# Attention on one Trainium2 core: GpSimd's sums, gathers and the loads in another order, and the row maxima turned by VectorE in 32x32 blocks and written by eight transfers

## The chip, the cores and the metric

The kernel runs on one core of a Trainium2 chip. The metric is the device time of one execution in microseconds. Measured three times, the kernel before took 1709.15 us in the median (1704.74 to 1709.72). A difference of 0.3% is about 5 us.

## The reference

Sixteen batches of 512 tokens with 256 features go through a layer norm, and three things are added: the input, block-sparse attention of the normed input, and a mixture of experts (16 experts, the two best for each token) with a shared expert.

```python
xn = _layernorm(x)                                   # x: [16, 512, 256]
qkv = (xn @ qkv_w.T)...                              # 16 heads of 16 features
block_mask = (c >= thresh) | eye(M)                  # M = 8 blocks of 64 tokens
scores = where(tmask, einsum('bhqd,bhkd->bhqk', q, k) * SCALE, -inf)
out = einsum('bhqk,bhkd->bhqd', softmax(scores), v)
x + (out @ proj_w.T + proj_b) + (routed + shared)
```

## The kernel before

There are three phases. `phase_front` norms the input, computes the shared expert, and sorts the tokens by expert. `phase_experts` computes the routed experts into `scratch_y`. `phase_attention` does the rest, and the change lies in it alone. It takes the time from about 590 us to the end.

**The unit of work.** A batch has 16 heads, in four groups (`q`) of four. A group is walked in eight steps (two heads and 128 tokens each), so a batch has 32 steps, `j` = 0 to 31. At a step TensorE makes two things. `st_pair` (L1599) multiplies keys with queries, transposed, for step j; ScalarE takes the exponential of it (`exp_pair`, L1409), and TensorE's `pv` (L1613) multiplies that with the values. `s_pair` (L1587) makes plain scores for the group two ahead; VectorE takes their row maxima (`max_pair`, L1449), 1024 columns at a time. Both use the three PSUM tiles of `ring` in turn.

**The row maxima.** The maxima have to be subtracted inside `st_pair`. So the query operand `stack[0]` has two rows more (`TOP0`, `TOP0 + 1`), the high and the low part of the maximum of each query, against rows of minus one on the key side. The maxima come out of VectorE with a query on each partition, and must lie along the free dimension of those two rows. Before, TensorE transposes them (`top_by_query`, L1555, 16x128 into the shared PSUM tile `ps_work`), VectorE splits them into two parts (`take_top`, L1458 and L1460), and two transfers of 8 KB write them into the stack (`top_rows`, L1201). The list `WORK` says at which step TensorE does which side job in `ps_work`: projections of the next batch (`qk`, `v`), the output by token (`o`), its transposition (`turn`), the output projection of the batch before (`final`) and the maxima (`top`, at j = 2, 10, 18, 26). Each job waits until the one before it has been taken out of `ps_work`.

**The queues.** Each engine's program is written out by hand in its order. SyncE (SP) issues nearly all transfers, in the order of its `body`: a transfer whose wait isn't over holds back all behind it. Once a batch SP does `store_out` of the batch before (L1207), then `load_part` (L1213, L1214), which first waits until that store has landed because it fills the same tile `part`, then `load_x`, and then `top_rows` for the first group of the next batch. GpSimd (POOL) splits q and k into two parts (`split`, L1299, L1301), does the same with the output (`split_on`, L1311, L1313), widens the mask (`widen`, L1284), gathers the experts' rows (`gather_y`, L1331, eight a batch), and adds them up (`add_y`: two weightings, L1339, and four sums into `part`, L1349). VectorE's `add_final` (L1484) waits for all six, and then adds the output projection.

```python
                if not first:
                    store_out(b - 1)
                    load_part(b)
                if not isinstance(b, int) or b + 2 < B:
                    load_x(b + 2)
                if not last:
                    top_rows(b + 1, d, 0)
```

The bodies of batches 0 to 3 and 13 to 15 are written out, those between are in a loop of three. The functions that the change touches:

## Time and profile before

| | |
|---|---|
| median of three runs | 1709.15 us (1704.74 to 1709.72) |
| the profiled execution's own time | 1708.7 us |
| its span in the profile | 1706.7 us |
| TensorE (PE) busy | 1383.7 us, 81% |
| VectorE (DVE) busy | 1035.2 us, 61% |
| ScalarE (ACT) busy | 868.0 us, 51% |
| GpSimd (POOL) busy | 781.8 us, 46% |
| mean granted TensorE clock | 0.912 |

The span is the time from the first to the last instruction. PEld is TensorE's loading of weights, beside the matmuls. A row of a group names the line, the engine, the operation, the tiles written and read, the count, the busy time with the mean of one in ns, and then the idle time of the engine before such instructions with what ended it. SPq is SyncE's issuing.

### The profile page before, as it was taken

Reading aid. Unit: us, or ns where it says so; the run is one execution under the profiler, and the core shown is the slowest. Engines: PE = TensorE matmul, PEld = TensorE weight load, DVE = VectorE, ACT = ScalarE, POOL = GpSimd, SP = SyncE. Lnnn points to the kernel's source line nnn. Section 1 sums busy time; section 2 is a strip of 40 time slices with the busy share of each in tenths; the row PEclk is TensorE's granted clock in tenths of the full one; section 3 lists DMA queues with packets and bytes.
Section 4 is the critical chain, followed back from the end, with each engine's and each line's share of the span. In section 5 each row is a group of like instructions: output and inputs, shape, how many; then the busy total and the mean of one; then the engine's idle time right before and its main releaser. Section 6 shows DMA issues by size and latency. Waiting matters only on the chain.

```text
span 1706.7 us, 28417 instructions
## 1 busy us (share of the span) xinstructions
PE 1383.7 (81%) x8618; PEld 812.8 (48%) x8619; DVE 1035.2 (61%) x1560; ACT 868.0 (51%) x1168; POOL 781.8 (46%) x778
## 2 busy tenths in 40 slices
PE   4988872398888647999898898899898898898984
PEld 3766651388888623443343343344343443443432
DVE  6876552455545408776676676676676776666660
ACT  4444420355555303666565565566565566555662
POOL 2577775022222321365364463463562663652645
PEclk9998985599999857999999999999998999998996
DMA  4666543344444355454554454445435635535411
GB/s 176 236 242 237 207 164 129 124 145 149 158 148 149 125 136 213 148 201 150 176 196 162 174 184 177 175 146 215 173 140 173 221 136 202 186 123 199 175 47 53
DMA packets 119722, 284.59 MB, mean 167 GB/s; under 512 B 16768, under 2 KB 52736, under 8 KB 111424
## 3 DMA queue, kind: packets, MB, share of 16 engines
q1 hardware_dynamic: 101568, 230.75, 38.8%
q0 software_dynamic: 18048, 52.45, 8.8%
q8 instruction: 64, 1.05, 0.2%
q14 instruction: 42, 0.34, 0.1%
HBM read 152.98 MB, written 129.11 MB: 165 GB/s over the span
## 4 chain that ended last, share of the span: by engine, by line
PE 21%; POOL 15%; DMA 14%; SPq 6%; issue 4%; ACT 2%; DVE 2%; POOLq 0%; DVEq 0%; ACTq 0%; another core or an unknown queue 0%
POOL at_part L1349 8%; DMA out<-at_part 8%; PE at_ps_pv L1613 7%; PE at_ring L1599 5%; PE at_ps_work L699 5%; DMA at_stack<-at_top_part 5%; POOL at_yg L1339 4%; PE at_ring L1587 3%; SPq L1168 2%; ACT at_pt L1409 1%; DVE at_top L1449 1%; DMA scratch_stack<-at_qk_part 1%; SPq L1222 1%; POOL at_qk_part L1301 1%; SPq L1201 1%
## 5 line engine op out<-in xcount | busy, mean ns | idle before, releaser
L1449 DVE TENSOR_REDUCE at_top<-at_ring 128x2 f32<-128x1024 f32 x512 | 624.7, 1223 | 321.2 <-PE at_ring L1587 295.1
L1409 ACT ACTIVATE at_pt<-at_ring 128x1024 f32<-128x1024 f32 x512 | 522.8, 1027 | 344.3 <-PE at_ring L1599 313.7
L1599 PE MATMUL at_ring<-at_stack 58*128 58x512 f32 x1024 | 260.8, 507 | 58.4 <-DMA at_stack<-at_top_part 51.3
L1613 PE MATMUL at_ps_pv<-at_pt,at_vx 128*32 128x512 f32 x2048 | 284.0, 628 | 4.4 <-ACT at_pt L1409 4.2
L1587 PE MATMUL at_ring<-at_stack 56*128 56x512 f32 x1024 | 228.7, 443 | 57.0 <-ACT at_pt L1409 25.1
L1599 PEld LDWEIGHTS at_ring<-at_stack 58*128 58x128 f32 x1024 | 98.1, 188 | 292.6 <-issue 196.8
L1331 POOL DMA_INDIRECT at_yg<-scratch_y,at_stage x128 | 123.5, 965 | 208.9 <-ACT at_pt L1409 174.9
L803 POOL DMA_DIRECT2D scratch_y<-ex_y x72 | 52.4, 727 | 223.0 <-ACT ex_y L841 219.0
L1299 POOL CAST at_qk_part<-at_qk_raw 128x512 fp32r<-128x512 f32 x64 | 39.2, 612 | 251.1 <-ACT at_qk_raw L1381 226.3
L284 POOL DMA_INDIRECT scratch_xs<-fr_xn,fr_slot x128 | 126.4, 988 | 56.0 <-issue 35.9
L1587 PEld LDWEIGHTS at_ring<-at_stack 56*128 56x128 f32 x1024 | 102.1, 196 | 96.8 <-ACT at_pt L1409 54.2
L699 PE MATMUL at_ps_work<-at_xh,qkv_part 128*128 128x512 f32 x256 | 106.7, 459 | 17.2 <-DMA at_xl<-scratch_xp 12.4
L880 DVE TENSOR_TENSOR ex_xl<-ex_ps_x,ex_xh 128x512 fp32r<-128x512 f32 x72 | 49.8, 691 | 80.9 <-ACT ex_xh L825 80.9
L699 PE MATMUL fr_ps_out<-fr_wd_part,fr_hh 128*128 128x256 f32 x256 | 57.0, 321 | 43.5 <-POOL fr_hl L276 41.5
L699 PE MATMUL ex_ps_gu<-ex_w_part,ex_xh 128*128 x288 | 88.3, 307 | 1.0 <-DVE ex_xl L880 0.7
L1301 POOL TENSOR_TENSOR at_qk_part<-at_qk_raw,at_qk_part 128x512 fp32r<-128x512 f32 x64 | 82.1, 1282 | 5.1
L699 PE MATMUL ex_ps_gu<-ex_w_part,ex_xl 128*128 x288 | 82.5, 287 | 0.0
L699 PE MATMUL ex_ps_gu<-ex_w,ex_xh 128*128 x288 | 82.4, 286 | 0.0
L1613 PEld LDWEIGHTS at_ps_pv<-at_pt,at_vx 128*32 128x32 f32 x2048 | 40.8, 109 | 86.9 <-issue 79.9
L1381 ACT COPY at_qk_raw<-at_ps_work 128x512 f32<-128x512 f32 x64 | 37.5, 587 | 85.9 <-PE at_ps_work L699 85.9
L699 PEld LDWEIGHTS at_ps_work<-at_xh,qkv_part 128*128 128x128 f32 x256 | 53.8, 210 | 57.4 <-DVE at_top_part L1460 16.0
L1349 POOL TENSOR_TENSOR at_part<-at_part,at_yg 128x1024 f32<-128x1024 f32 x32 | 76.2, 2383 | 2.5
(204 smaller groups left out, 2463.3 us busy)
## 6 DMA issues: line engine op xcount, KB each, us to landing
at_stack<-scratch_stack SPq DMA_DIRECT2D x64, 1024.0 KB, 6.3
scratch_stack<-at_qk_part SPq DMA_DIRECT2D x192, 256.0 KB, 2.6
ex_xg<-scratch_xs SPq DMA_DIRECT2D x144, 128.0 KB, 2.1
scratch_y<-ex_y POOLq DMA_DIRECT2D x72, 256.0 KB, 3.1
fr_x_in<-in_x SPq DMA_DIRECT2D x16, 512.0 KB
scratch_xp<-fr_xh SPq DMA_DIRECT2D x16, 512.0 KB
scratch_xp<-fr_xl SPq DMA_DIRECT2D x16, 512.0 KB
scratch_part<-fr_part SPq DMA_DIRECT2D x16, 512.0 KB
```

Of the source, the lines that this page charges most:

```text
L284: nc.gpsimd.indirect_dma_start(out=dram["xs"], out_offset=bass.IndirectOffsetOnAxis(ap=slot[:, j, c:c + 1], axis=0), in_=xn[b % XN][:, t, ...
L699: ins = nc.tensor.matmul(out, a, b, start=(first and n == 0), stop=(last and n == len(todo) - 1))
L803: nc.gpsimd.dma_start(dram["y"][bass.ds(at, 2 * P), :].rearrange("(u p) d -> p u d", p=P), y[i][:]).then_inc(y_stored[i], 16)
L1301: nc.gpsimd.tensor_tensor(qk_part[s][1][:], qk_raw[s][:], f32(qk_part[s][0][:]), ALU.subtract).then_inc(split_ready, 1)
L1331: nc.gpsimd.indirect_dma_start(out=yg[j][:, t, :], out_offset=None, in_=dram["y"], in_offset=bass.IndirectOffsetOnAxis(ap=stage[:, j, t:t ...
L1339: nc.gpsimd.tensor_tensor(yg[j][:], yg[j][:], keep["weight"][:, j, bass.ds(TB * b, TB)].unsqueeze(2).broadcast_to([P, TB, D]), ALU.mult).t ...
L1349: nc.gpsimd.tensor_tensor(part[:], part[:], term, ALU.add).then_inc(added, 1)
L1409: nc.scalar.activation(pt[t][:, 2 * pair:2 * pair + 2, :], st_slot(c, j)[:], ACT.Exp, scale=float(HD) ** -0.5).then_inc(exp_ready, 1)
L1449: v.tensor_reduce(cols[:, :, TB * pair + t], slot[0][:], AX, ALU.max).then_inc(s_max, 1)
L1587: last = nc.tensor.matmul(slot[:, half, :], stack[0][r][rows, pl, t * P:(t + 1) * P], stack[1][r][rows, pl, :], start=True, stop=True)
L1599: last = nc.tensor.matmul(slot[:, half, :], stack[1][r][rows, pl, t * P:(t + 1) * P], stack[0][r][rows, pl, :], start=True, stop=True)
L1613: last = nc.tensor.matmul(ps_pv[2 * HD * g:2 * HD * (g + 1), :], vx[c][:, t, G * q + g, :], pt[t][:, g, :], start=(t == 0), stop=(t == TB ...
```

## The change

- The maxima no longer go through TensorE. `turn_top` on VectorE splits the [128, 16] tile into high and low (128x16 each), and turns the [128, 32] result in 32x32 blocks (one instruction). It comes right after the eighth maximum of a group. The block form leaves pieces of 32 queries, so `top_rows` now issues eight transfers of 128-byte pieces instead of two of 512-byte ones.
- `WORK` loses its four `top` entries a batch.
- `load_x` has three buffers and is moved up, behind the first stack load. `load_part` loses the load of x, which becomes `load_rows`, one batch ahead. `store_mask` and `widen` are moved from the batch's start to the end of the batch before.
- On GpSimd the four sums into `part` are split up: x and the bias are added to the first gathered tile (`add_x`) within the same batch, and only one weighting and two sums are left for the next batch's start. The gathers are spread between the other work.

```diff
+    TOPS = 16 * 2 * (P // 32)
-    WORK = ((1, "qk", 0), (2, "top", 0), (3, "qk", 1), (5, "o", 0), (7, "turn", 0), (9, "turn", 1), (10, "top", 1),
...
+    WORK = ((1, "qk", 0), (3, "qk", 1), (5, "o", 0), (7, "turn", 0), (9, "turn", 1), (11, "qk", 2), (13, "o", 1),
...
-        xh, xl = sb("xh", [P, KD, N], F32R), sb("xl", [P, KD, N], F32R)
+        xh = [sb(f"xh{i}", [P, KD, N], F32R) for i in range(RING)]
+        xl = [sb(f"xl{i}", [P, KD, N], F32R) for i in range(RING)]
...
             def top_rows(b, c, q):
-                sp.wait_ge(top_low, ready)
+                sp.wait_ge(turned, ready)
                 pairs = slice((q % 2) * 2, (q % 2) * 2 + 2)
                 for x in range(2):
-                    sp.dma_start(f32(stack[0][group(c, q)][TOP0 + x::64, pairs, :]).rearrange("e r n -> e (r n)"),
-                                 f32(top_part[q % 2][:, x, :])).then_inc(top_here[q % 2], 16)
+                    for a in range(P // 32):
+                        rows = 32 * a + G * TB * x
+                        sp.dma_start(f32(stack[0][group(c, q)][TOP0 + x::64, pairs, :]).rearrange(
+                            "e r (t a n) -> e (r t) a n", t=TB, a=P // 32)[:, :, a],
+                            top_turned[q % 2][rows:rows + G * TB]).then_inc(top_here[q % 2], 16)
...
             def body(b, c, first=False, last=False):
                 d = (c + 1) % 3
+                counts = mask_counts(b + 2)
                 top_rows(b, c, 1)
                 if not last:
-                    store_mask(b + 1, d)
                     store_qk(b + 1, d, 0)
                     store_qk(b + 1, d, 1)
                     load_stack(b + 1, d, 0)
+                if not isinstance(b, int) or b + 2 < B:
+                    load_x(b + 2, (c + 2) % 3)
                 top_rows(b, c, 2)
...
                 if not first:
                     store_out(b - 1)
-                    load_part(b)
+                load_part(b)
+                if not last:
+                    load_rows(b + 1)
                 if not isinstance(b, int) or b + 2 < B:
-                    load_x(b + 2)
+                    store_mask(b + 2, (c + 2) % 3, counts)
                 if not last:
                     top_rows(b + 1, d, 0)
...
+                if not first:
+                    weigh_y(b - 1, 1)
                 if not last:
-                    widen(b + 1)
                     split(b + 1, 0)
+                if not first:
+                    add_y(b - 1, 1)
+                if not last:
                     split(b + 1, 1)
                 if not first:
+                    add_y(b - 1, 0)
                     split_on(b - 1, 0)
+                stage_rows(b)
+                gather_y(b, 0, 0, 8)
+                if not first:
                     split_on(b - 1, 1)
-                    add_y(b - 1)
+                gather_y(b, 0, 1, 11)
                 if not last:
                     split(b + 1, 2)
+                gather_y(b, 0, 2, 14)
+                gather_y(b, 0, 3, 15)
+                if not last:
                     split(b + 1, 3)
-                gather_y(b)
+                weigh_y(b, 0)
+                add_x(b)
+                gather_y(b, 1, 0, 20)
+                if not isinstance(b, int) or b + 2 < B:
+                    widen(b + 2)
+                for t in range(1, TB):
+                    gather_y(b, 1, t, 20 + 3 * t)
...
-            def take_top(u, q, past_use):
+            def turn_top(u, q, past_use):
                 i = q % 2
-                dve.wait_ge(top_in_psum, u + 1)
+                dve.wait_ge(s_max, HALF * u + HALF)
+                if past(u, 2):
+                    dve.wait_ge(turned, u - 1)
+                v.tensor_copy(top_part[i][:, 0, :], top[i][:]).then_inc(top_high, 1)
+                dve.wait_ge(top_high, u + 1)
+                v.tensor_tensor(top_part[i][:, 1, :], top[i][:], f32(top_part[i][:, 0, :]), ALU.subtract).then_inc(top_low, 1)
                 if past_use is not None:
                     dve.wait_ge(top_here[i], past_use)
...
+                dve.wait_ge(top_low, u + 1)
+                v.transpose(top_turned[i][:], f32(top_part[i][:]).rearrange("p x c -> p (x c)")).then_inc(turned, 1)
```

How the rows stand on the engines. First SP's queue, from the store of a batch's output on; the row of L1201 holds the maxima of two groups, two transfers each. Before:

```order
L1193 DMA at_stack<-scratch_stack 128x2048 x2
L1207 DMA out<-at_part 128x1024
L1213 DMA at_part<-scratch_part 128x1024
L1214 DMA at_x_in<-in_x 128x1024
L1153 DMA at_xh<-scratch_xp 128x1024
L1153 DMA at_xl<-scratch_xp 128x1024
L1201 DMA at_stack<-at_top_part 2x8x128 x4
L1181 DMA scratch_stack<-at_wide 32x512 x4
L1168 DMA scratch_stack<-at_qk_part 64x2x512 x6
```

The same place of the changed kernel:

```order
L1205 DMA at_stack<-scratch_stack 128x2048 x2
L1222 DMA out<-at_part 128x1024
L1228 DMA at_part<-scratch_part 128x1024
L1235 DMA at_x_in<-in_x 128x1024
L1193 DMA scratch_stack<-at_wide 32x512 x4
L1215 DMA at_stack<-at_top_turned 2x8x32 x16
L1175 DMA scratch_stack<-at_qk_part 64x2x512 x6
L1205 DMA at_stack<-scratch_stack 128x2048 x2
L1160 DMA at_xh<-scratch_xp 128x1024
L1160 DMA at_xl<-scratch_xp 128x1024
L1215 DMA at_stack<-at_top_turned 2x8x32 x8
```

Between the store and the first group's maxima, the two loads of the next x have gone and the four of the mask have come; the maxima are eight transfers to a group.

Next GpSimd at the start of a batch, from the first split of the next batch's queries on. Before:

```order
L1299 CAST at_qk_part<-at_qk_raw 128x512
L1301 TENSOR_TENSOR at_qk_part<-at_qk_raw,at_qk_part 128x512
L1299 CAST at_qk_part<-at_qk_raw 128x512
L1301 TENSOR_TENSOR at_qk_part<-at_qk_raw,at_qk_part 128x512
L1311 CAST at_on_part<-at_on_raw 128x512
L1313 TENSOR_TENSOR at_on_part<-at_on_raw,at_on_part 128x512
L1311 CAST at_on_part<-at_on_raw 128x512
L1313 TENSOR_TENSOR at_on_part<-at_on_raw,at_on_part 128x512
L1339 TENSOR_TENSOR at_yg<-at_yg,weight 128x1024 x2
L1349 TENSOR_TENSOR at_part<-at_part,at_x_in 128x1024
L1349 TENSOR_TENSOR at_part<-at_part,at_bias 128x1024
L1349 TENSOR_TENSOR at_part<-at_part,at_yg 128x1024 x2
```

And now:

```order
L1363 TENSOR_TENSOR at_yg<-at_yg,weight 128x1024
L1325 CAST at_qk_part<-at_qk_raw 128x512
L1327 TENSOR_TENSOR at_qk_part<-at_qk_raw,at_qk_part 128x512
L1382 TENSOR_TENSOR at_part<-at_part,at_yg 128x1024
L1325 CAST at_qk_part<-at_qk_raw 128x512
L1327 TENSOR_TENSOR at_qk_part<-at_qk_raw,at_qk_part 128x512
L1382 TENSOR_TENSOR at_part<-at_part,at_yg 128x1024
L1337 CAST at_on_part<-at_on_raw 128x512
L1339 TENSOR_TENSOR at_on_part<-at_on_raw,at_on_part 128x512
L1348 COPY at_stage<-slot 128x8
L1355 DMA at_yg<-scratch_y,at_stage 128x256
```

Six long operations behind the splits of the output have become three ahead of them; the other three stand later in the batch before.

## Rows read from the trace of the kernel before

**Rows 1.** The page: span and busy time of each engine.

```profile
span 1706.7 us, 28417 instructions
PE 1383.7 (81%) x8618; PEld 812.8 (48%) x8619; DVE 1035.2 (61%) x1560; ACT 868.0 (51%) x1168; POOL 781.8 (46%) x778
```

**Rows 2.** Windows, batches 1 to 14: us, busy times, granted clock, DMA share, GB/s.

```profile
714.28:1625.00 910.72, 813.09 (x4986) 369.93 (x4986) 621.80 (x701) 538.10 (x618) 465.57 (x430) 0.95 0.49 174
```

**Rows 3.** Waits of the same stretch: us in total, times, the longest.

```profile
PE at_ring L1599 <- DMA at_stack<-at_top_part: 51.3, 12, 6.9
DVE at_part L1484 <- POOL at_part L1349: 21.1, 14, 1.6
DVE at_top L1449 <- remote: 17.6, 9, 2.2
PE at_ps_work L699 <- DVE at_top_part L1460: 9.8, 17, 0.7
```

**Rows 4.** Timeline of SP's queue at the end of batch 8: start, us.

```profile
1214.52 1.38 SPq L1193 DMA_DIRECT2D at_stack<-scratch_stack  x2
1216.11 0.42 SPq L1207 DMA_DIRECT2D out<-at_part  x1
1225.87 0.34 SPq L1213 DMA_DIRECT2D at_part<-scratch_part  x1
...
1227.83 1.09 SPq L1201 DMA_DIRECT2D at_stack<-at_top_part  x2
```

**Rows 5.** The chain that ended last, at the same place: start, us.

```profile
1216.11 9.61 DMA out<-at_part
1228.41 6.50 DMA at_stack<-at_top_part
```

**Rows 6.** Timeline of PE, the first step of batch 9.

```profile
1234.95 0.50 PE L1599 MATMUL at_ring<-at_stack 58*128 58x512 f32 x2 [3.41 <-DMA at_stack<-at_top_part]
```

**Rows 7.** Window just behind that wait, columns as in rows 2.

```profile
1237.50:1239.50 2.00, 2.00 (x7) 1.16 (x6) 1.12 (x1) 1.34 (x2) 0.00 (x0) 0.51 0.03 8
```

**Rows 8.** Timeline of ACT: exponentials of j = 0 and 2, batches 9 and 11.

```profile
1235.58 1.03 ACT L1409 ACTIVATE at_pt<-at_ring 128x1024 f32<-128x1024 f32 x1 [3.21 <-PE at_ring L1599]
1241.06 1.03 ACT L1409 ACTIVATE at_pt<-at_ring 128x1024 f32<-128x1024 f32 x1
1366.36 1.02 ACT L1409 ACTIVATE at_pt<-at_ring 128x1024 f32<-128x1024 f32 x1 [1.08 <-PE at_ring L1599]
1370.31 1.03 ACT L1409 ACTIVATE at_pt<-at_ring 128x1024 f32<-128x1024 f32 x1
```

**Rows 9.** Groups by line: sums, weightings, the maxima's transposition, small VectorE operations.

```profile
L1349 POOL TENSOR_TENSOR at_part<-at_part,at_yg 128x1024 f32<-128x1024 f32 x32 | 76.2, 2383 | 2.5
L1339 POOL TENSOR_TENSOR at_yg<-at_yg,weight 128x1024 f32<-128x1024 f32 x32 | 59.9, 1894 | 1.8 <-DMA at_yg<-scratch_y,at_stage 1.8
L1555 PE MATMUL at_ps_work<-ident,at_top 128*16 128x128 f32 x64 | 17.8, 278 | 8.9 <-DVE at_part L1484 7.2 <-DVE at_top L1449 1.6
L1458 DVE CAST at_top_part<-at_ps_work 16x128 fp32r<-16x128 f32 x64 | 17.7, 276 | 5.0 <-remote 2.2 <-PE at_ps_work L1555 1.2
L452 DVE TENSOR_TENSOR fr_carry<-fr_carry,fr_upto 128x16 f32<-128x16 f32 x8 | 1.5, 190 | 0.3
```

**Rows 10.** Issues by line on SP: ns least/median/most.

```profile
L1201 SPq DMA_DIRECT2D at_stack<-at_top_part x128: 495/532/618, 650.9 to 1658.9; - x128
L1222 SPq DMA_DIRECT2D scratch_stack<-at_block_of x6: 882/1288/1303, 598.0 to 616.1; - x6
```

**Rows 11.** Timeline of SP's queue: the masks of one batch.

```profile
1244.32 1.74 SPq L1181 DMA_DIRECT2D scratch_stack<-at_wide  x4
```

**Rows 12.** The page's DMA issues: KB each, us to landing.

```profile
scratch_stack<-at_qk_part SPq DMA_DIRECT2D x192, 256.0 KB, 2.6
```

**Rows 13.** Timelines of POOL and PE after the last step.

```profile
1678.70 3.75 POOL L1339 TENSOR_TENSOR at_yg<-at_yg,weight 128x1024 f32<-128x1024 f32 x2 [1.83 <-DMA at_yg<-scratch_y,at_stage]
...
1696.13 2.90 PE L699 MATMUL at_ps_work<-proj_part,at_on_part 128*128 128x256 f32 x12 [11.76 <-POOL at_on_part L1313]
```

161 lines of the change are left out of this document (84 added, 77 removed).

## The prediction

> **What bounds the kernel now.** I read the page first: TensorE (PE) is busy for 81% of the span [rows 1]. Within batches 1 to 14 it is 813 of 911 us, or 89% [rows 2], VectorE 68% and GpSimd 51%. A batch takes 910.72 / 14 = 65.05 us. So TensorE is the bound inside a batch, and about 98 us of these 911 are its own gaps. The waits tell what ends the gaps [rows 3]: TensorE waits 51.3 us, in 12 batches of 14, for the maxima's transfer into the stack at a batch's first step. VectorE waits 21.1 us, 14 times, for GpSimd's sums before it can add the output projection; meanwhile no row maxima are taken. TensorE waits 9.8 us for VectorE to clear the transposed maxima out of the shared tile. The 17.6 us that VectorE waits for "remote" are no work of this program's engines, and I leave them as they are.
>
> Why the maxima come late is read from SP's queue and the chain. In batch 8 the store of the output is issued at 1216.11, and the load behind it stands until 1225.87 [rows 4], since the store takes 9.61 us to land [rows 5]. Four loads follow, 2 MB together, and only then, at 1227.83, the maxima [rows 4]. These 8 KB transfers land 6.50 us after 1228.41 [rows 5]: the ring works in order, and they queue behind the loads. TensorE has then stood 3.41 us [rows 6]. Right afterwards its granted clock is 0.51, the 1.2 GHz level [rows 7], so that the first two steps take 1241.06 - 1235.58 = 5.48 us in batch 9; in batch 11, where ScalarE waited only 1.08 us, the same two take 1370.31 - 1366.36 = 3.95 us [rows 8].
>
> **The change, part by part.** All sums are made against the profiled execution, 1708.7 us, which is 0.45 us under the median of the three; I treat them as the same.
>
> *A, the wait at the batch's start: -51.3 us* [rows 3]. This is the whole of it; what comes back is F.
>
> *B, the slow clock behind it: -18 us.* 5.48 - 3.95 = 1.53 us [rows 8], 12 times.
>
> *C, the sums before the output projection: -17 us.* Before, a weighting pair and four sums take 2 x 1.89 + 4 x 2.38 = 13.3 us [rows 9] behind `split_on`. Now 1.89 + 2 x 2.38 = 6.7 us stand at the batch's start, spread between the splits, and the output projection is at j = 17, about 30 us into the batch. Their finish should lie near 13 us (weighting, split, sum, split, sum). So the 21.1 us go; I take four fifths, because part of such a wait is slack for TensorE. The other 6.7 us move to the middle of the batch before. GpSimd's cover is large (51% busy), and its gathers need their rows only at the end of the batch.
>
> *D, the transposition off TensorE: -14 us.* Per batch four matmuls of 0.278 us [rows 9] go, 14 x 4 x 0.278 = 15.6 us on the engine that bounds, and the 9.8 us of waits [rows 3]. The bounds are 9.8 and 25.4 us. I take 14, as the side job behind each transposition also loses the switch, but the steps around it wait partly for ScalarE.
>
> *E, the work on VectorE: +8 us.* The old pair is 16x128, 0.276 us the first of them [rows 9], about 0.55 together. The new operations are 128x16, 128x16 and a turn of 128x32. The nearest row is a 128x16 sum of 0.190 us [rows 9], so the three are 0.57 us if the turn costs as much, and 0.66 if it costs the 0.276 of the old cast. By itself that is nothing. But the set stands right behind the eighth maximum, and in steps 5 to 9 VectorE has five maxima, an output and this set in hardly more time than they need. I take 0.6 us a batch, 14 x 0.6 = 8. Bounds: 0, and all of it uncovered, 14 x 4 x 0.65 = 36 us. The Trainium skill ("VectorE: DVE Perf Modes", The three transpose paths) says that VectorE turns 32x32 blocks only, and gives 311 ns for a 128x128 bf16 tile. With this as the turn's price the sum would be up to 14 x 4 x 0.12 = 7 us higher. No row here shows a turn.
>
> *F, what is left of the wait at the start: +10 us.* The store still stands ahead of the first group's maxima on SP, and `load_part` still waits for its landing. From the store's issue on: 9.6 to land [rows 5], 0.8 for two loads' issue, masks 1.74 [rows 11], eight transfers at 0.53 [rows 10] with gaps 4.4, and landing. No row shows an 8 KB transfer alone; the bounds are 2.6 us [rows 12] and 6.5 [rows 5], from the issue. I take 2, since only 1 MB of loads and 0.25 MB of masks are ahead now and these drain while the eight are issued. That is 18.5 us from the store to the landing. What is there: from 1216.11 to the time the first step could have begun, 1234.95 - 3.41 = 1231.54 [rows 4, 6], are 15.4 us. The store goes out earlier, as the last split isn't behind the sums any more (some 5 us), and later by six more issues for the fourth group (3.2 us): 17.2 us. It falls short by 1.3, of which I count 0.7 a batch, as any late step inside the batch is time given. A wait of 1 us did not bring the slow clock [rows 8]. 14 x 0.7 = 10 us. Bounds: 0, and 3 us with the slow clock, 14 x 4.5 = 63.
>
> *The other groups' maxima* are in time. Those of the third group are issued behind 2 MB of stack and now 1 MB of x; they are due at j = 16, about 10 us after the stack load. That leaves 1 to 2 us, and I cost it at nothing. If it fails, each us is 14 us. `load_x` is off the path, with two batches of time. `store_mask` and `widen` are a batch ahead, 1.74 us of SP that moves from the split to the late end of the batch (in F).
>
> *The end: -10 us.* After the last step GpSimd's sums [rows 13] run ahead of TensorE's last projections, which wait 11.76 us for it. 13.3 becomes 6.7 us: -7. The last batch has its own wait of kind C: -3.
>
> Sum: 51 + 18 + 17 + 14 + 10 - 8 - 10 = 92 us, and 1708.7 - 92 = 1616.7, so **1617 us**. A batch then takes some 59 us.
>
> **Rivals.**
>
> *R1: SP's queue sets the pace in part.* 32 transfers a batch instead of 8 at up to 0.618 us each [rows 10] and a store that lands a us later make F 2.5 us with the slow clock's 1.5, 4 x 14 = 56 instead of 10: 1663 us. For it: SP stands in one order, and the wait for the store stays. Against: the x loads leave the place where they hurt. The Trainium skill ("DMA: Bandwidth & Descriptors", Specifications) gives 512 B as the least piece for full rate, with a read-modify-write below; pieces go from 512 to 128 B. By this rule the landing would be longer, on the side of R1. Chance 0.15.
>
> *R2: VectorE becomes the bound* around the ends of the groups, with E at its upper bound of 36: 1617 + 28 = 1645 us. For it: its steps are full near j = 5 to 9. Against: 68% on the whole [rows 2], and the old pair goes. Chance 0.10.
>
> *R3, slower: a short transfer takes as long to issue as the constants' rows.* These are 64 KB, also written in three-dimensional pieces, and took 1.288 us each in the median [rows 10]. Between the last split and the first group's landing stand 16 of the new ones, so each 0.1 us more costs 1.6 us a batch. At 1.29 the wait would be 0.7 + 16 x 0.76 + 1.5 = 14.4 us: 14 x 14.4 = 201 instead of 10, 1808 us. All gains of 102 us are eaten at 7.3 us a batch, that is from 0.85 us per transfer. Against: the form is the same as of the old maxima (2x8 pieces), which took 0.532, only with shorter pieces. Chance 0.08.
>
> *R4: nothing measurable*, because the time moves into waits for "remote" or for the third group's maxima: 1709 us. Chance 0.03.
>
> **How the numbers follow.** The forecast has 0.64. Its own range is from 1588 (E and F at 0, D at its upper bound, 1617 - 8 - 10 - 11) to 1640. The 80% range goes from 1588 to 1662: it takes in R2 and half of R1, and leaves out R3 and what is under. About 0.3%, or 5 us, is what a measurement of this kernel can tell from no change. Faster: 0.64 + 0.15 + 0.10 = 0.89; same 0.03; slower 0.08.
>
> **What would show it.** Right: the windows of batches 1 to 14 near 59 us each; PE's wait for the maxima's tile under 15 us in all; the granted clock near 1 throughout these batches; no VectorE wait for GpSimd before L1542; SP's issues of L1215 at 0.5 to 0.6 us; the three VectorE operations near 0.2 us each. Wrong: issues of L1215 above 0.85 us; the store's landing above 11 us; or a wait of TensorE for the maxima at j = 16 or 24, which I cost at nothing.

## The result and the profile after

| | before | after |
|---|---|---|
| median of four runs each, same chip | 1707.24 us | 1578.52 us (1577.34 to 1586.24) |
| ratio | | 0.9256 [0.9222, 0.929] |
| span of the profiled execution | 1706.7 us | 1575.7 us |
| mean granted TensorE clock | 0.912 | 0.938 |

The change is worth 128.7 us between the medians and 131.0 us between the two profiled spans. I had forecast 92, and the time lies under the range's lower end of 1588.

The page of after, span and busy time of each engine, beside [rows 1]:

```profile
span 1575.7 us, 28883 instructions
PE 1333.9 (85%) x8554; PEld 791.4 (50%) x8555; DVE 1047.4 (66%) x1624; ACT 868.3 (55%) x1168; POOL 784.8 (50%) x778
```

The window of batches 1 to 14 of after, beside [rows 2] (us, busy times, granted clock, DMA share, GB/s):

```profile
704.93:1502.19 797.26, 769.75 (x4928) 355.61 (x4928) 630.14 (x757) 538.00 (x618) 468.38 (x431) 0.99 0.56 199
```

A batch takes 797.26 / 14 = 56.95 us instead of 65.05. TensorE is busy for 97% of it (before 89%), the granted clock is 0.99 (before 0.95), and TensorE's own gaps fell from 98 to 27.5 us. VectorE's and GpSimd's work hardly changed.

Three of the waits of the same stretch of after, TensorE and VectorE, beside [rows 3]:

```profile
DVE at_part L1542 <- PE at_ps_work L699: 12.0, 28, 0.5
PE at_ring L1637 <- ACT at_pt L1463: 9.7, 16, 0.7
PE at_ring L1649 <- DMA at_stack<-at_top_turned: 9.5, 9, 3.0
```

TensorE's wait at the batch's start fell from 51.3 to 9.5 us, VectorE's wait for GpSimd's sums (21.1) is gone and so is its "remote" (17.6). The timeline of SP's queue of after at the end of batch 8, beside [rows 4]:

```profile
1140.93 0.97 SPq L1205 DMA_DIRECT2D at_stack<-scratch_stack  x2
1142.10 0.35 SPq L1222 DMA_DIRECT2D out<-at_part  x1
1150.81 0.34 SPq L1228 DMA_DIRECT2D at_part<-scratch_part  x1
1151.83 0.00 SPq L1235 DMA_DIRECT2D at_x_in<-in_x  x1
1151.95 1.77 SPq L1193 DMA_DIRECT2D scratch_stack<-at_wide  x4
1153.77 8.72 SPq L1215 DMA_DIRECT2D at_stack<-at_top_turned  x11
```

The last row holds the first group's eight issues and, behind a pause, those of the second. The first step of batch 9 follows in TensorE's timeline, and then the window around it (columns as in the window above), beside [rows 6, 7]:

```profile
1159.16 0.49 PE L1649 MATMUL at_ring<-at_stack 58*128 58x512 f32 x2 [0.27 <-DMA at_stack<-at_top_turned]
```

```profile
1157.00:1163.00 6.00, 5.62 (x35) 2.25 (x34) 5.71 (x10) 4.57 (x5) 1.90 (x1) 1.00 0.09 24
```

So the maxima are in the stack 1159.16 - 1142.10 = 17.1 us after the store was issued. At this batch TensorE stands 0.27 us and not 3.41, and its granted clock stays at 1.00, the 2.4 GHz level. The eight issues, from the view of line L1215 (least/median/most ns):

```profile
L1215 SPq DMA_DIRECT2D at_stack<-at_top_turned x512: 495/495/792, 640.7 to 1537.2; - x171
```

The groups by line of after, VectorE, batches 1 to 14 (busy us, mean ns | idle before):

```profile
L1503 DVE TENSOR_REDUCE at_top<-at_ring 128x2 f32<-128x1024 f32 x449 | 546.0, 1223 | 143.5 <-PE at_ring L1637 128.5 <-issue 9.7
...
L1514 DVE TENSOR_TENSOR at_top_part<-at_top,at_top_part 128x16 fp32r<-128x16 f32 x56 | 16.1, 287 | 1.9
...
L1512 DVE CAST at_top_part<-at_top 128x16 fp32r<-128x16 f32 x56 | 12.8, 229 | 1.9
L1519 DVE STREAM_TRANSPOSE at_top_turned<-at_top_part 128x32 f32<-128x32 f32 x56 | 11.8, 212 | 5.9
```

The three new operations take 229 + 287 + 212 = 728 ns a group in the mean. Their usual durations are shorter: in the trace the median is 175 ns for the cast, 175 for the subtraction and 211 for the turn, 561 together. The means are raised by 24 casts and subtractions of the whole program that took 263 to 2381 ns, and every one of these ended 27 to 31 ns after an instruction of GpSimd. `packed_free` below shows what that can cost.

The timeline of after behind the last steps, beside [rows 13]:

```profile
1558.87 2.35 POOL L1382 TENSOR_TENSOR at_part<-at_part,at_yg 128x1024 f32<-128x1024 f32 x1 [0.18 <-POOL at_part L1382]
...
1565.15 2.90 PE L699 MATMUL at_ps_work<-proj_part,at_on_part 128*128 128x256 f32 x12 [3.54 <-POOL at_on_part L1339]
```

GpSimd's last sum ends at 1561.22, beside TensorE's last transpositions, and TensorE waits 3.54 us instead of 11.76.

**Where the time went.** A step is the time between the starts of two exponentials of ScalarE in the timeline. Summed over batches 1 to 14, with the other profile of each kernel (both on one other chip, see the end of the experiments):

| us | before | after | gain | before, again | after, again |
|---|---|---|---|---|---|
| up to the first exponential | 658.5 | 649.5 | 9.0 | 641.3 | 640.6 |
| batch 0 | 55.8 | 55.5 | 0.3 | 55.8 | 55.0 |
| 1 to 14, start (j = 31, 0, 1) | 151.1 | 90.6 | 60.5 | 184.1 | 95.4 |
| 1 to 14, old side jobs of the maxima (j = 2, 3, 10, 11, 26, 27) | 160.7 | 145.3 | 15.4 | 159.0 | 145.3 |
| 1 to 14, output projection (j = 17 to 19) | 104.4 | 86.3 | 18.1 | 104.5 | 86.3 |
| 1 to 14, j = 20 to 25 | 171.5 | 153.1 | 18.4 | 153.4 | 153.1 |
| 1 to 14, the others | 323.0 | 321.9 | 1.1 | 321.3 | 321.6 |
| batch 15 | 51.7 | 53.0 | -1.3 | 60.6 | 47.7 |
| behind the last exponential | 30.0 | 20.5 | 9.5 | 28.4 | 20.5 |

The gains sum up to 131.0 us.

Two starts are long even where nothing waits for the maxima: those into batches 7 and 10, where the loop of three batches turns. In `part_last` below, which has no such wait, the other starts take 5.3 to 5.5 us and these two 9.3 and 9.2, with TensorE idle for 2.97 and 2.87 us in waits that the profile calls "issue". The row is 83.2 us there, and I take this as its floor.

### The profile page after: what moved, and what is told of

Read it like the earlier page. It is cut to its first block and busy times, and to the rows that moved or that the text cites. A ratio compares the mean times of both kernels' runs of the same rounds, so it can differ in the third digit from the quotient of the medians.

```text
span 1575.7 us, 28883 instructions
## 1 busy us (share of the span) xinstructions
PE 1333.9 (85%) x8554; PEld 791.4 (50%) x8555; DVE 1047.4 (66%) x1624; ACT 868.3 (55%) x1168; POOL 784.8 (50%) x778
## 5 line engine op out<-in xcount | busy, mean ns | idle before, releaser
L1663 PE MATMUL at_ps_pv<-at_pt,at_vx 128*32 128x512 f32 x2048 | 277.7, 615 | 4.3 <-ACT at_pt L1463 4.2
L1649 PE MATMUL at_ring<-at_stack 58*128 58x512 f32 x1024 | 256.4, 498 | 21.7 <-DMA at_stack<-at_top_turned 9.5
L1637 PE MATMUL at_ring<-at_stack 56*128 56x512 f32 x1024 | 223.9, 433 | 48.0 <-DMA at_stack<-scratch_stack 28.2
L699 PE MATMUL at_ps_work<-at_xh,qkv_part 128*128 128x512 f32 x256 | 100.1, 432 | 14.3 <-DMA at_xl<-scratch_xp 12.2
L1363 POOL TENSOR_TENSOR at_yg<-at_yg,weight 128x1024 f32<-128x1024 f32 x32 | 60.6, 1895 | 41.1 <-DMA at_yg<-scratch_y,at_stage 41.1
```

The source lines that it names most:

```text
L699: ins = nc.tensor.matmul(out, a, b, start=(first and n == 0), stop=(last and n == len(todo) - 1))
L1363: nc.gpsimd.tensor_tensor(yg[j][:], yg[j][:], keep["weight"][:, j, bass.ds(TB * b, TB)].unsqueeze(2).broadcast_to([P, TB, D]), ALU.mult).t ...
L1637: last = nc.tensor.matmul(slot[:, half, :], stack[0][r][rows, pl, t * P:(t + 1) * P], stack[1][r][rows, pl, :], start=True, stop=True)
L1649: last = nc.tensor.matmul(slot[:, half, :], stack[1][r][rows, pl, t * P:(t + 1) * P], stack[0][r][rows, pl, :], start=True, stop=True)
L1663: last = nc.tensor.matmul(ps_pv[2 * HD * g:2 * HD * (g + 1), :], vx[c][:, t, G * q + g, :], pt[t][:, g, :], start=(t == 0), stop=(t == TB ...
```

## The experiments

The theory to be tested: SP's queue with all that holds it back (GpSimd's last split, the store, the loads ahead) decides when the maxima land; the orders earn the time, and the eight transfers cost issue time. The rival: taking the transposition off TensorE earns a good part by itself. Ratios are to runs of the kernel before on the same chip.

### Each half of the change by itself

`max_only` is the kernel before with the maxima turned on VectorE and written by eight transfers, and no order changed but the entries of `WORK`.

```diff
-            (11, "qk", 2), (13, "o", 1), (15, "qk", 3), (17, "final", 0), (18, "top", 2), (19, "final", 1), (21, "o", 2),
-            (23, "v", 0), (25, "v", 1), (26, "top", 3), (29, "o", 3))
+            (15, "qk", 3), (17, "final", 0), (19, "final", 1), (21, "o", 2), (23, "v", 0), (25, "v", 1), (29, "o", 3))
...
+                        if j % HALF == HALF - 1:
+                            turn_top(Q * b + q + 2, q, TOPS * (2 * b + q // 2 + 1))
```

> The kernel before with the new way of the maxima alone (turn on VectorE, eight transfers, no transposition on TensorE); all orders of GpSimd and SP as before. Theory 1 (the order of the queues made the gain, and the maxima's way is worth only the work taken off TensorE): minus 15 us for that; the wait at the batch's start stays, because SP still stands at the store, and grows by the six more issues of the fourth group (3.3 us) ahead of the store: 14 x 3.3 = plus 46. 1707 - 15 + 46 = 1738 us, and TensorE waits near 90 us for the maxima's tile. Theory 2 (the maxima's way is the gain, since they are ready earlier): 1707 - 15 - 51 = 1640 us, with the wait under 15 us.

Measured: 1714.83 us, 1.0105 [1.005, 1.016]: this half by itself makes the kernel 1.0% slower. Theory 1 had 31 us more than before and it was 20, so that theory is the nearer one. Its waits in batches 1 to 14:

```profile
PE at_ring L1600 <- DMA at_stack<-at_top_turned: 116.5, 28, 7.8
DVE at_part L1493 <- POOL at_part L1354: 27.3, 14, 2.0
SPq L1170 <- POOL at_qk_part L1306: 312.0, 41, 15.3
```

TensorE waits twice a batch. The second place, which neither theory had, shows in its timeline (the rows with this wait around batch 8's start, the first one at j = 24 of batch 7):

```profile
1143.90 0.50 PE L1600 MATMUL at_ring<-at_stack 58*128 58x512 f32 x2 [2.55 <-DMA at_stack<-at_top_turned]
...
1163.05 0.80 PE L1600 MATMUL at_ring<-at_stack 58*128 58x512 f32 x2 [6.71 <-DMA at_stack<-at_top_turned]
```

SP issues the fourth group's maxima behind the last store of q and k, which waits for GpSimd's last split, and that stands behind the sums. Eight issues instead of two no longer fit behind it. The steps of the old side jobs did fall to 145.3 us, as in after, but steps 20 to 25 rose to 201.4 and the start took 177.0. The steps 17 to 19 fell too, from 104.4 to 87.9 us, although GpSimd's sums stayed where they were: with `top` at j = 18 gone, the job at j = 19 no longer waits for a maxima's job that had itself waited for the first half of the output projection. This is the wait in the kernel before, batches 1 to 14:

```profile
PE at_ps_work L1555 <- DVE at_part L1484: 4.1, 12, 0.4
```

`pe_turn` is the other half: after, with the old way of the maxima (TensorE's transposition, two transfers).

```diff
-                for x in range(2):
-                    for a in range(P // 32):
...
+                    sp.dma_start(f32(stack[0][group(c, q)][TOP0 + x::64, pairs, :]).rearrange("e r n -> e (r n)"),
+                                 f32(top_part[q % 2][:, x, :])).then_inc(top_here[q % 2], 16)
```

> The changed kernel with the maxima turned on TensorE and written by two transfers, as before; the new orders stay. Theory 1: plus 15 us for the four side jobs a batch on TensorE, minus the 9.5 us that TensorE still waits for the maxima's tile, as 24 issues a batch are gone: 1578 + 15 - 9 = 1585 us. Theory 2 (the maxima's way is the gain): the wait at the batch's start returns, plus 60 and more: 1640 us or above. If the eight transfers were a burden on the whole, it would be faster than the changed kernel, 1570 us.

Measured: 1579.17 us, 0.9313 [0.9267, 0.936]. The window of its batches 1 to 14:

```profile
695.64:1507.22 811.58, 785.88 (x4984) 359.68 (x4984) 623.81 (x701) 536.81 (x618) 467.85 (x431) 0.99 0.54 195
```

No wait for the maxima is left. TensorE is busy 16.1 us longer than in after, about the 15.6 of the 56 transpositions, and the side jobs' steps are back at 159.0 us, 13.7 above. The steps 17 to 19 take 90.4 us, 4.1 above. The start takes 87.2 us, 3.4 less than in after. The two halves are not additive: the orders alone give 0.931, the maxima alone 1.011, and both together 0.925 to 0.926. The maxima's new way pays some 11 us by these ratios, whose intervals overlap, and 10 to 14 us by the windows (811.6 against 801.7 and 797.3), and only where SP has time for its issues.

### What of the orders it is

`sums_late`: after, with GpSimd in its old order (all sums at the start behind `split_on`, gathers packed at the end; `widen` stays at the end too, now behind all gathers). `load_rows` has to go one batch later with `add_x`.

```diff
-                if not first:
-                    weigh_y(b - 1, 1)
                 if not last:
                     split(b + 1, 0)
...
+                    weigh_y(b - 1, 0)
+                    add_x(b - 1)
+                    weigh_y(b - 1, 1)
+                    add_y(b - 1, 1)
+                    add_y(b - 1, 0)
                 if not last:
                     split(b + 1, 2)
                     split(b + 1, 3)
```

> The changed kernel with GpSimd's old order: both weightings and four sums behind the two splits of the output, all gathers behind the last split of the queries. Theory 1: VectorE's wait for the sums returns (18 us over j = 17 to 19), the pause at j = 20 to 25 returns (18), the end is 7 us later, and the last split comes some 5 us later, which delays the store and brings back the wait at the batch's start: 4 us with the slow clock, 14 x 4 = 56. 1578 + 99 = 1677 us. Rival (the moved loads of x alone repaired the batch's start): 18 + 18 + 7 only, 1621 us.

Measured: 1756.01 us, 1.0349 [1.0297, 1.0402], much slower than expected. Its waits in batches 1 to 14:

```profile
PE at_ring L1640 <- DMA at_stack<-at_top_turned: 142.3, 28, 9.4
DVE at_part L1533 <- POOL at_part L1380: 31.8, 14, 2.4
SPq L1188 <- POOL at_wide L1308: 47.5, 13, 5.0
```

VectorE's wait for the sums is back (31.8 us), and both of TensorE's places as in `max_only`. My expectation had left out the place at j = 24. It is slower than `max_only` too, because the mask's store, moved to the batch's end, now waits there for GpSimd, ahead of the first group's maxima (start 206.1 us against 177.0). So in this arrangement the moved loads and masks earn nothing by themselves. They need GpSimd's new order. The old order with `widen` at its old place and only the loads moved was not run.

`gathers_packed`: only the spreading of the gathers is undone. The first four come behind the last split, at steps 16 to 22, so that the weighting, `add_x` and `widen` behind them come later.

```diff
-                stage_rows(b)
-                gather_y(b, 0, 0, 8)
                 if not first:
                     split_on(b - 1, 1)
-                gather_y(b, 0, 1, 11)
...
+                stage_rows(b)
+                for t in range(TB):
+                    gather_y(b, 0, t, 16 + 2 * t)
                 weigh_y(b, 0)
                 add_x(b)
```

> The changed kernel with the first four gathers back to back behind the last split; the sums stay in the new order. In the kernel before ScalarE and VectorE pause at j = 21 and 22 although their input is there, while a 16 KB packet of the instruction queue is under way. Theory 1 (the packed gathers hold up that packet): steps 20 to 25 take 18 us more over the batches, 1596 us. Rival (the pause came from the late sums): no change at those steps, 1578 to 1583 us.

Measured: 1697.17 us, 1.001 [0.9984, 1.0035]: the whole gain is gone, from GpSimd work that no other compute engine waits for. Waits of its batches 1 to 14:

```profile
PE at_ring L1646 <- DMA at_stack<-at_top_turned: 112.2, 14, 9.3
SPq L1188 <- POOL at_wide L1310: 54.3, 13, 4.3
SPq L1235 <- POOL at_yg L1374: 43.5, 14, 3.7
```

Neither theory had this. The output projection stayed at 86.4 us and steps 20 to 25 at 153.0, so the pause did not come back with the packed gathers. Nearly all of the loss is at the start, 205.4 us against 90.6 (and 8 in batch 0). SP stands for the mask that `widen` makes and for the tile that `add_x` reads, and the first group's maxima stand behind both. `packed_free` tests this reading: the same GpSimd order, but SP issues the first group's maxima ahead of those two.

```diff
                 load_part(b)
                 if not last:
+                    top_rows(b + 1, d, 0)
                     load_rows(b + 1)
                 if not isinstance(b, int) or b + 2 < B:
                     store_mask(b + 2, (c + 2) % 3, counts)
-                if not last:
-                    top_rows(b + 1, d, 0)
```

> The kernel with the packed gathers (1697 us) and one more edit: SP's two transfers that wait for GpSimd (the load of x for the sums, the mask) stand behind the first group's maxima. Theory 1 (packing the gathers made add_x and widen late, and SP, standing in order at those two, held back the maxima; the gathers themselves cost nothing): the wait at the batch's start falls back to that of the changed kernel or under, 1560 to 1590 us. Rival (the packed gathers fill the ring or delay the store): it stays above 1650 us.

Measured: 1596.06 us, 0.939 [0.9355, 0.9424], 6 us above the range of Theory 1. The start falls from 205.4 to 86.9 us, and TensorE's wait for the maxima to:

```profile
PE at_ring L1645 <- DMA at_stack<-at_top_turned: 4.9, 4, 2.8
```

These four are at j = 16, where the third group's maxima are due; none is at a batch's start. SP still waits 41.7 us for the mask, now with nothing urgent behind it. Of the 128 us between `gathers_packed` (1697.17) and the changed kernel (1569.22 beside `part_last`) 101 come from one place in one queue. (They ran on different chips, on which the kernel before took 1695 to 1698 us.) What is left against after, 24 us in batches 1 to 14, lies mostly at j = 9 (36.1 us against 19.5). There TensorE waits for a maximum, and its releaser is late for this reason, read from the waits and from the timelines of GpSimd and VectorE in batch 8:

```profile
PE at_ring L1645 <- DVE at_top L1499: 17.2, 11, 2.1
```

```profile
1122.60 2.39 POOL L1381 TENSOR_TENSOR at_part<-at_part,at_yg 128x1024 f32<-128x1024 f32 x1
```

```profile
1123.15 1.87 DVE L1508 CAST at_top_part<-at_top 128x16 fp32r<-128x16 f32 x1
```

The cast, 0.175 us otherwise, lasts until GpSimd's sum is over: it ends at 1125.02, 27 ns behind it. In seven of the 14 batches the cast at j = 8 took 1.0 to 2.2 us, and each time it ended 27 to 34 ns after this sum. So a sum of GpSimd that meets VectorE's set behind the eighth maximum holds up the maxima, and then TensorE.

`x_late`: only `load_x` goes back ahead of the first group's maxima.

```diff
-                if not isinstance(b, int) or b + 2 < B:
-                    load_x(b + 2, (c + 2) % 3)
                 top_rows(b, c, 2)
...
                     store_mask(b + 2, (c + 2) % 3, counts)
+                if not isinstance(b, int) or b + 2 < B:
+                    load_x(b + 2, (c + 2) % 3)
                 if not last:
                     top_rows(b + 1, d, 0)
```

> The changed kernel with the loads of x where they were, right ahead of the first group's maxima. Theory 1 (the maxima queue in the ring behind what is loaded in front): 1 MB more ahead costs at most 2.5 us and 0.7 us of issue, against the 4.4 us in which the eight are issued anyway, so 1 to 2 us a batch with some slow clock: plus 14 to 35 us. Rival (only the wait for the store's landing counts): plus 10 us at most, the issue alone.

Measured: 1612.61 us, 0.9515 [0.9476, 0.9555], or 43 us above the changed kernel on the same chip (1569.22). The wait of batches 1 to 14:

```profile
PE at_ring L1649 <- DMA at_stack<-at_top_turned: 43.5, 13, 4.7
```

The wait grew by 43.5 - 16.1 = 27.4 us against `after_again`, and the granted clock of batches 1 to 14 fell from 0.99 to 0.95; the start steps grew by 44.7 us. The other 17.3 I put down to the slow clock, 1.3 us for each of 13 waits, near the 1.53 that the prediction had for B. This expectation had left only about 0.5 us for it under its upper end of 35. In the ring too the maxima were later: they landed 2.5 us in the median after the last issue, against 1.54.

### The eight transfers and VectorE

`sixteen` writes each piece by two transfers of 1 KB, so 64 issues a batch.

```diff
+                        for h in range(2):
+                            sp.dma_start(f32(stack[0][group(c, q)][TOP0 + x::64, pairs, :]).rearrange(
+                                "e r (t a n) -> e (r t) a n", t=TB, a=P // 32)[:, :, a, 16 * h:16 * h + 16],
+                                top_turned[q % 2][rows:rows + G * TB, 16 * h:16 * h + 16]).then_inc(top_here[q % 2], 16)
```

> The changed kernel with each of the eight transfers cut into two of 64-byte pieces: 64 issues a batch instead of 32. Theory 1 (SP's issues are the price, 0.5 us each; the first group is late at once, the fourth group and the store by the fourth group's eight): 16 more between the last split and the first group's landing, 8 us a batch with 1.5 us of slow clock, plus 130 us. Rival (the issues are hidden, only the landing of the last counts): plus 4 us a batch, 56 us.

Measured: 1718.73 us, 1.0129 [1.0092, 1.0166], 149.5 us above the changed kernel on the same chip. The issues over the whole program, and the waits of batches 1 to 14:

```profile
L1216 SPq DMA_DIRECT2D at_stack<-at_top_turned x1024: 495/495/997, 631.8 to 1677.1; - x171
```

```profile
PE at_ring L1650 <- DMA at_stack<-at_top_turned: 134.1, 27, 10.5
```

The price is 149.5 / 14 = 10.7 us a batch for 32 issues more, so 0.33 us each: part of the 0.495 still falls into SP's free time (its wait for GpSimd's splits fell from 162.9 us in `after_again` to 81.2). Of TensorE's 27 waits 14 are at a batch's start and 13 at j = 16, for the third group, where Theory 1 had named the fourth. This is the mechanism of R3, brought about by number instead of length. Sixteen issues of 0.495 are as long as eight of 0.99, which is past my threshold of 0.85 us, and the kernel is indeed slower than before. Where the threshold lies this one point doesn't show.

`turn_more` adds three more turns a group on VectorE, whose result nothing uses.

```diff
+                for k in range(3):
+                    if k or past(u, 1):
+                        dve.wait_ge(more, 3 * u + k)
+                    v.transpose(extra[:], f32(top_part[i][:]).rearrange("p x c -> p (x c)")).then_inc(more, 1)
                 v.transpose(top_turned[i][:], f32(top_part[i][:]).rearrange("p x c -> p (x c)")).then_inc(turned, 1)
```

> The changed kernel with three more turns of the maxima (0.21 us each, in a chain) on VectorE for each group: 2.8 us more a batch. Theory 1 (VectorE has slack, as no step beside the maxima grew): TensorE goes on as before, but the maxima come 0.7 us later, which costs nothing where SP stands at the store anyway: plus 0 to 10 us. Rival (VectorE is as full around the ends of the groups as the prediction counted): 14 x 2 to 2.8, plus 28 to 40 us, in the steps 7 to 9, 15 to 17, 23 to 25 and 31 to 1.

Measured: 1583.74 us, 0.9309 [0.9275, 0.9344]. Its groups by line and one of its waits, batches 1 to 14:

```profile
L1523 DVE STREAM_TRANSPOSE at_extra<-at_top_part 128x32 f32<-128x32 f32 x168 | 35.6, 212 | 14.2 <-DVE at_top_part L1515 8.6
```

```profile
PE at_ring L1654 <- DVE at_top L1504: 10.1, 15, 1.3
```

35.6 us more work (and 14.2 us of idling around it) cost 811.7 - 801.7 = 10.0 us in these batches, and 14.5 us between the medians, between the two theories. Of the 10.0, 7.4 are at j = 9 (26.9 against 19.5), among the steps 5 to 9 that the prediction named. So at the end of one of the four groups the cover of VectorE is just about used up by the change: its own set was free, and what comes on top is not. At the ends of the other groups there is no such loss; the start took 3.5 us more.

### The same kernels again, and two better ones

> The changed kernel once more, unaltered, beside the kernel before on this chip. Whatever the chip: batches 1 to 14 take 797 us within 1%, as all of this is the attention's order. The two phases ahead of the attention are the same in both kernels: if the 9 us by which the first exponential came earlier in the changed kernel's profile (649.5 against 658.5) is chance of the run, it moves now; if it came with the change, it stays near 649.

Measured: 1569.22 us, 0.9248 [0.9214, 0.9282]. It agrees with the first ratio. Batches 1 to 14 took 801.7 us, within the 1%, and the first exponential came at 640.6. The chip is faster (before 1696.37 there), and TensorE's wait for the maxima is 16.1 us in 11 batches.

> The kernel before once more, unaltered, for a profile on this chip. If the pause of ScalarE and VectorE at j = 21 and 22 (18 us over batches 1 to 14, absent from every other profile of this study) belongs to this program, it is there again and steps 20 to 25 take near 171 us; if it was chance of one execution, they take near 153 and the batches 1 to 14 near 893 us. The first exponential should come near 650 us if the phases ahead differ by the program, near 640 if by the chip.

A single execution of the kernel before, 1710.55 us. It is longer than any of the other eight beside it (1693.82 to 1704.39, median 1697.93), and its batches 1 to 14 took 922.4 us, not the 893 expected. The waits of its batches 1 to 14:

```profile
PE at_ring L1599 <- DMA at_stack<-at_top_part: 79.4, 13, 7.6
DVE at_part L1484 <- POOL at_part L1349: 21.1, 14, 1.6
```

There is no "remote", and steps 20 to 25 take 153.4 us, as in every kernel without the second late place. But the start takes 184.1 us instead of 151.1. A 16 KB packet of the instruction queue, which `gathers_packed` suspected, begins at j = 21 or 22 in the same nine batches of both profiles, so it does not make the pause by itself. So of the two reasons for TensorE's gaps in my trace, one belonged to that execution, and the other is larger where it is missing.

`part_last` moves the load that waits for the store behind the first group's maxima.

```diff
                 if not first:
                     store_out(b - 1)
-                load_part(b)
...
                 if not last:
                     top_rows(b + 1, d, 0)
+                load_part(b)
```

> The changed kernel with the load of the partial sums put behind the first group's maxima on SP, so that these no longer stand behind the store's landing. Theory 1 (what is left of TensorE's wait at the batch's start, 9.5 us, is SP standing at the store): the wait goes, and the few us of slow clock, 1 to 2 us a batch in steps 31, 0 and 1: batches 1 to 14 in 780 to 788 us, 10 to 15 us less than the changed kernel. Rival (the wait comes from the rate of the ring, or the late load delays the sums at the next batch's start): no gain, or a new wait of VectorE for the sums at j = 17.

Measured: 1560.66 us, 0.9191 [0.9162, 0.9219], with batches 1 to 14 in 789.5 us. The waits for the transfer of the maxima are gone from TensorE's list. SP's waits in batches 1 to 14, of which the second was 117.6 us in after:

```profile
SPq L1215 <- DVE at_top_turned L1519: 141.4, 28, 9.0
...
SPq L1228 <- DMA out<-at_part: 6.3, 8, 1.5
```

Now SP waits for the maxima to be computed, and no longer the maxima for SP. `all_last` moves the rows' load and the mask's store behind them too.

```diff
+                if not last:
+                    top_rows(b + 1, d, 0)
                 load_part(b)
                 if not last:
                     load_rows(b + 1)
...
-                if not last:
-                    top_rows(b + 1, d, 0)
```

> The changed kernel with the partial sums' load, the x load for the sums and the masks all behind the first group's maxima; only the store stays ahead. Theory 1 (nothing but SP's order delays these maxima): they are issued as soon as they are turned, j = 23 to 24, and the batch's start has no wait: as the kernel with only the partial sums' load moved, or 0 to 5 us less. Rival (the maxima of the second group, turned at the batch's end, now stand behind masks and loads and make the queue late for the next splits): 5 to 15 us more than that kernel.

Measured: 1559.03 us, 0.9176 [0.9149, 0.9202], which can't be told from `part_last`. Both beat the changed kernel, by 9 to 10 us on the same chip; `part_last` was run beside it.

## Why the prediction was wrong

The direction was right, and so was the mechanism at the start of a batch. The sum was 39 us short (131.0 of the spans against 92). By its own steps, against the table above:

*A, B and F, the start:* forecast 51.3 + 18 - 10 = 59.3, measured 60.5. F was 0.7 us a batch, or 10, and the row of the wait reads 9.5. Against the floor of 83.2 us that `part_last` has there, A and B were worth 151.1 - 83.2 = 67.9 (forecast 69.3) and F cost 7.4. The parts behind it hold as well: 17.1 us from the store's issue to the landing (forecast 18.5, as the store landed in 8.7 us at most instead of 9.6, and the issues took 0.495 instead of 0.53), of which 16.8 were there (forecast 17.2). The landing, which no row showed, took 1159.16 - 1157.6 = 1.6 us from the last issue, under my bounds of 2.6 and 6.5.

*C, the sums, and D, the transposition:* forecast 17 + 14 = 31, measured 18.1 at j = 17 to 19 and 15.4 at the side jobs' steps, 33.5. That each number is close to its own term is partly luck. The 18.1 belong to both terms: `pe_turn`, with the sums moved and the transposition kept, gains 14.0 of them, and `max_only`, with the transposition gone and the sums kept, 16.5. `top` stood at j = 18 between the two halves of the output projection, in one chain of waits for `ps_work`, and either half of the change breaks that chain. With the maxima's new way in place the new orders are worth only 1.6 us more there (`max_only` against after), or 6.1 (`sums_late` against after). The prediction added the two as independent terms. Taking the transposition back in `pe_turn` cost 13.7 us at the side jobs' steps and 4.1 here.

*E, VectorE:* forecast +8, measured nothing. **This step failed** as the prediction put it, "I take 0.6 us a batch". By themselves the three operations take 0.56 us a group, about the 0.57 of the estimate; in the mean it was 0.73, since some had to wait for GpSimd, which the sum didn't have. No step from j = 2 to 30 grew by more than 0.5 us over the 14 batches against before's second profile, though. `turn_more` shows why it wasn't foolish: the next 0.64 us a group do cost, at the place named. So does a sum of GpSimd that meets the set (`packed_free`, 16.6 us at j = 9). The lower bound was the right value.

*The "remote" wait:* **this step failed**, "are no work of this program's engines, and I leave them as they are". It is the largest miss, 18.4 us at j = 20 to 25 [rows 3]. I left it in the new kernel as if it were a property of the program. It shows in the profile of one execution of before, and in none of the other 13 profiles, in before's second one neither. In that second one the wait at the start is larger by 28.1 us (79.4 against 51.3). So A's row, too, held only part of what SP's chain costs. My reading, argued and not tested by itself, is that the pause fell into time that was lost anyway: where SP's chain sets the length of a batch, what holds TensorE at j = 21 shortens the wait at j = 0. Within the first profile the batches lean that way: the six with more than 12.4 us at j = 20 to 25 are followed by starts of 10.1 us in the mean, the seven with less by 12.1; in the second profile, with 11.0 in every batch, the starts take 13.5. But the second profile is also of an execution slower than all others beside it, so the 28.1 are no clean measure. What the pause was is not settled. A gap from outside should have been priced at both of its ends, staying or going, in the range.

*The part ahead of the attention:* 9.0 us of the gain are in code that the change doesn't touch. The other profiles of both kernels, both on one other chip, have 641.3 and 640.6 there, and those of all the experiments 637.8 to 644.5. So nothing shows that the 9.0 come with the change, and I take them as chance of that pair.

*The other groups' maxima*, costed at nothing: right for the changed kernel, but only due to the sums' new place. With the sums in their old place, the fourth group is late once a batch (`max_only`, `sums_late`). The third group's maxima did queue behind the loads, and landed 5 to 6.5 us after the last issue in most batches of after, still in time.

*The end:* forecast -7 for the tail and -3 for the last batch; measured -9.5 and +1.3.

The differences: 1.2 + 1.1 + 1.4 + 9.1 (E, with the 1.1 of the other steps) + 18.4 + 9.3 (first phases and batch 0) - 1.8 = 38.7, and 0.3 is rounding of the forecast's sum. Without the two failed steps the forecast would have been 1617 - 8 - 18 = 1591, and the lower end of the range, which held E at 0 but never the pause's going, 1588 - 18 = 1570, under the 1578.5 measured.

*The rivals.* R1 asked for 4 us a batch left at the start, and 0.7 were left of the wait. Its mechanism is real, as `x_late` (43 us) and `gathers_packed` (all of the gain) show, but the changed orders stay just on the right side of it. The rule that I cited for it, from the Trainium skill ("DMA: Bandwidth & Descriptors", Specifications), that pieces below 512 B lose rate, doesn't show here: with nothing ahead of them, 2 KB in pieces of 128 B landed 1.54 us after the last issue, 1 KB in pieces of 64 B (`sixteen`) 1.52, and 8 KB in pieces of 512 B (`pe_turn`) 1.7. All of these go from SBUF to SBUF and are small. No run varies the length of the pieces alone, or that of a transfer to or from HBM. With 64 B the price of each further transfer was 0.33 us, less than its issue alone. R2 was not met, but `turn_more` and `packed_free` show it near, at one place of a batch. R3's price did not come, since a short piece is issued in 0.495 us, no slower than the old 512-byte one (0.532 [rows 10]); `sixteen`, beyond its threshold, is slower than before as R3 says. R4 is out.

*The turn:* it measured 212 ns for 128x32 in f32. The Trainium skill ("VectorE: DVE Perf Modes", The three transpose paths) has 311 ns for a 128x128 bf16 tile. With that price I would have added up to 7 us to a term that turned out to be none.

## What to carry to other kernels

Follow each queue that issues in order as a chain with its own length a batch: all that is ahead of the urgent transfer counts, and so does whatever those issues wait for, on whichever engine. GpSimd at half load cost, with one order of its work, 101 us as the releaser of two transfers that stood ahead of the maxima. At the batch's start, moving the urgent transfer ahead of them was as good as making GpSimd early (86.9 us against 90.6).

Waits at different places of one period do not add up where they hang on one chain: each half of the change gained most of the same 18 us at j = 17 to 19. Where the chain is that of another engine, this is likely too, but here it is argued from two profiles. A wait that no engine of the program explains may be gone in the next execution: give it both prices in the range.

More and smaller transfers are paid in issue time, and this costs only when the queue has no time left; so count the free time of the queue first. The same half of this change made the kernel some 11 us faster or 18 us slower depending on it.

## What the runs showed of the hardware that was not expected

- A transfer of 2 KB in pieces of 128 B is issued in 0.495 us, one of 8 KB in pieces of 512 B in 0.532, and one of 1 KB in pieces of 64 B in 0.495 as well: with 16 pieces each, the issue's length hardly depends on their bytes, unlike the 1.288 us of the constants' rows [rows 10], which have 32 pieces of 2 KB. Alone they landed 1.54, 1.7 and 1.52 us after the last issue; the same 2 KB behind 3 MB of loads landed after 5 to 6.5 us.
- A cast or subtraction of VectorE on 128x16 from SBUF takes 0.175 us, or lasts until an instruction of GpSimd is over. In after, all 24 of more than 0.25 us ended 27 to 31 ns behind one of GpSimd, the longest at 2.38 us. In before, the same two operations read PSUM: 74 of 128 overlapped a GpSimd operation on two tensors, and none took more than 0.28 us.
- VectorE turns 128x32 f32 in 212 ns, and in 170 ns right behind three others of the kind. It is less than the old cast of a 16x128 tile (276 ns [rows 9]).
- The wait of TensorE has a price beyond itself through its clock: in `x_late` 27 us more of waiting made the start steps 45 us longer, with the granted clock of batches 1 to 14 at 0.95 instead of 0.99.
